# Layer 0's head of a two-layer attention and MLP kernel: a new order for the first three batches, with batch 1's second value product, batch 2's turns and three of batch 1's high halves placed behind the first raw tiles

## What is computed

```python
mod = (_silu(L0_c) @ L0_wmod).reshape(L0_c.shape[0], 6, 1, -1)
h = _layernorm(x, axis=-1) * (1 + ca) + sa
q = (x @ wq.T).reshape(B, T, H, hd)        # x is h here; k and v likewise
q, k = (rms(q), rms(k))                    # g_rms * (t * rsqrt(mean(t * t) + EPS))
q, k = (rope(q), rope(k))
scores = jnp.einsum('bhtd,bhsd->bhts', qh, kh) * scale + 1.0
attn = jax.nn.softmax(scores, axis=-1)
y = jnp.einsum('bhts,bhsd->bhtd', attn, vh)
```

## Time and profile before

| | |
|---|---|
| median of 3 runs | 1977.23 us (1971.51 to 1978.44) |
| the profiled execution | 1978.1 us, span 1976.4 us |
| mean granted clock of PE | 0.961 |
| PE busy | 1824.8 us, 92% of the span |
| DVE, ACT, POOL busy | 1338.8, 1140.3, 660.1 us |
| first raw tile, first scores | 82.25 us, 109.43 us |
| last scores of layer 0's attention | about 560 us |

### The profile page before, as it was taken

How to read it: one execution, slowest core, us unless ns; L and a number is a source line. 1 busy time by engine, 2 the same in 40 slices (tenths; PEclk the granted TensorE clock), 3 DMA queues, 4 the chain that set the end, 5 groups by cost and what they waited for, 6 DMA issues and landing times. The chain is left out here.

```text
span 1976.4 us, 29572 instructions
## 1 busy us (share of the span) xinstructions
PE 1824.8 (92%) x10382; PEld 757.2 (38%) x10382; DVE 1338.8 (68%) x2599; ACT 1140.3 (58%) x1536; POOL 660.1 (33%) x920
## 2 busy tenths in 40 slices
PE   4789999998979999999999997799999998799998
PEld 3333333332224444444444443223332322455554
DVE  5479888888834535535445352688888885689983
ACT  4368788876743424334234242577777777467674
POOL 5657777772220000000000111334433312446452
PEclk8679999999989999999999999799999999799999
DMA  3345544444243000000001003233332222433410
GB/s 119 64 93 124 131 120 115 113 102 113 92 171 148 22 1 22 22 1 22 22 0 48 1 22 65 51 77 64 74 72 59 61 54 69 158 128 133 160 43 33
DMA packets 119620, 147.65 MB, mean 75 GB/s; under 512 B 19779, under 2 KB 102838, under 8 KB 117430
## 3 DMA queue, kind: packets, MB, share of 16 engines
q1 hardware_dynamic: 119478, 145.79, 27.9%
HBM read 100.34 MB, written 45.14 MB: 74 GB/s over the span
## 5 line engine op out<-in xcount | busy, mean ns | idle before, releaser
L854 DVE TENSOR_REDUCE A_M<-A_SM 128x1 f16<-128x512 f32 x1024 | 654.1, 683 | 136.4 <-PE A_SM L1069 133.9
L625 ACT ACTIVATE A_P<-A_ST 128x1024 f32<-128x1024 f32 x512 | 523.9, 1026 | 165.7 <-PE A_ST L1085 158.0
L1069 PE MATMUL A_SM<-A_KT,A_QS 48*128 48x512 f16 x1024 | 353.0, 397 | 45.7 <-DVE A_M L854 38.1
L1627 PE MATMUL B_PA<-B_Hh,B_wh 128*128 128x512 f16 x1024 | 388.1, 379 | 0.0
L1627 PE MATMUL B_PA<-B_Hl,B_wh 128*128 128x512 f16 x1024 | 388.1, 379 | 0.0
L1546 ACT ACTIVATE B_af<-B_PA,B_sv 128x512 f32<-128x512 f32 x192 | 132.0, 688 | 353.6 <-PE B_PA L1627 353.4
L1085 PE MATMUL A_ST<-A_QS,A_KT 49*128 49x512 f16 x1024 | 299.0, 385 | 3.0 <-DMA A_QS<-A_rows 2.4
L1102 PE MATMUL A_AV<-A_P,A_V 128*32 128x512 f32 x2048 | 274.9, 609 | 4.2 <-ACT A_P L625 3.6
L1069 PEld LDWEIGHTS A_SM<-A_KT,A_QS 48*128 48x128 f16 x1024 | 83.1, 93 | 431.3 <-DVE A_M L854 381.3
L1590 DVE TENSOR_SCALAR B_Hh<-B_af 128x512 f16<-128x512 f32 x128 | 59.0, 461 | 279.3 <-ACT B_af L1546 279.3
L1341 POOL TENSOR_TENSOR B_hl<-B_hf,B_hh 128x512 f16<-128x512 f32 x14 | 16.2, 1156 | 506.2 <-ACT B_hh L1357 506.2
(11 more groups left out here) (365 smaller groups left out, 3273.2 us busy)
## 6 DMA issues: line engine op xcount, KB each, us to landing
D_w_st<-in_we_dram SPq DMA_DIRECT2D x16, 1024.0 KB, 5.0
qk<-A_tr SPq DMA_DIRECT2D x58, 256.0 KB, 2.5
A_KT<-qk SPq DMA_DIRECT2D x96, 128.0 KB, 5.1
A_QS<-qk SPq DMA_DIRECT2D x96, 128.0 KB, 4.6
A_w_st<-in_w_ffn_dram SPq DMA_DIRECT2D x32, 352.0 KB, 3.3
A_QS<-A_rows SPq DMA_DIRECT2D x512, 0.5 KB
w_hi<-A_f_hi SPq DMA_DIRECT2D x32, 176.0 KB, 3.5
w_lo<-A_f_lo SPq DMA_DIRECT2D x32, 176.0 KB, 3.8
```

The lines of the kernel that those rows point to most:

```text
L625: nc.scalar.activation(P[:, st, 2 * pair:2 * pair + 2, :], ST[:, u % 2, :, :], ACT.Exp, scale=1.0 / math.sqrt(HD)).then_inc(exp_s, 1)
L854: nc.vector.tensor_reduce(M[G % 2][:, o:o + 1], SM[:, n % 2, :], AX, ALU.max, negate=True).then_inc(max_s, 1)
L1069: nc.tensor.matmul(SM[:, n % 2, :], QS[b % 2][r, 2 * g + pair, tt * 128:tt * 128 + 128], KT[b % 2][r, 2 * g + pair, :], start=True, stop=T ...
L1627: ins = nc.tensor.matmul(out, a, c, start=start and kt == 0 and n_ == 0, stop=stop and kt == kts[-1] and n_ == len(ops) - 1)
```

## The change

Only numbers in two tables are changed. No operation is added or removed, and none changes its size or engine.

```diff
-                            H0=30, H1=31, H2=32, H3=33, HIGH=(36, 36, 36, 36, 37, 37, 37, 37), LOWS=(38, 38, 38, 38))),
-          placed(-140, dict(STAT=(10, 10, 10, 10), AGG=11, ROOT=11, XN=(16, 16, 16, 16), T0=21, T1=23, HH=(22, 24), HL=(23, 25),
...
+                            H0=24, H1=25, H2=26, H3=27, HIGH=(31, 31, 31, 31, 32, 32, 32, 32), LOWS=(33, 33, 33, 33))),
+          placed(-140, dict(STAT=(10, 10, 10, 10), AGG=11, ROOT=11, XN=(16, 16, 16, 16), T0=18, T1=19, HH=(18, 19), HL=(19, 20),
...
```

More of the change, by code:

```diff
@@ L135 @@
                             INV=(14, 17), ROT=(16, 16, 17, 17), HI=(17, 18, 19, 20), LOW=(18, 19, 20, 21),
-                            H0=30, H1=31, H2=32, H3=33, HIGH=(36, 36, 36, 36, 37, 37, 37, 37), LOWS=(38, 38, 38, 38))),
-          placed(-140, dict(STAT=(10, 10, 10, 10), AGG=11, ROOT=11, XN=(16, 16, 16, 16), T0=21, T1=23, HH=(22, 24), HL=(23, 25),
-                            QK0=25, QK1=26, QK2=27, QK3=28, V0=40, V1=42, SUM=(29, 29, 34, 35), VAR=(30, 34), RMSG=(31, 35),
-                            INV=(32, 37), ROT=(33, 36, 48, 50), HI=(37, 39, 128, 133), LOW=(38, 40, 129, 134),
+                            H0=24, H1=25, H2=26, H3=27, HIGH=(31, 31, 31, 31, 32, 32, 32, 32), LOWS=(33, 33, 33, 33))),
+          placed(-140, dict(STAT=(10, 10, 10, 10), AGG=11, ROOT=11, XN=(16, 16, 16, 16), T0=18, T1=19, HH=(18, 19), HL=(19, 20),
+                            QK0=20, QK1=21, QK2=22, QK3=23, V0=30, V1=127, SUM=(29, 29, 34, 35), VAR=(30, 34), RMSG=(31, 35),
+                            INV=(32, 37), ROT=(33, 36, 48, 50), HI=(37, 132, 133, 134), LOW=(38, 46, 133, 135),
                             H0=137, H1=139, H2=140, H3=141, HIGH=(143, 143, 144, 144, 145, 145, 146, 146), LOWS=(147, 147, 148, 148))),
-          placed(-140, dict(STAT=(35, 35, 36, 36), AGG=37, ROOT=37, XN=(41, 41, 41, 41), T0=44, T1=46, HH=(45, 47), HL=(46, 47))),
+          placed(-140, dict(STAT=(28, 28, 28, 28), AGG=28, ROOT=29, XN=(30, 30, 30, 30), T0=129, T1=131, HH=(129, 131), HL=(130, 132))),
           placed(-140, dict(STAT=(127, 128, 130, 131), AGG=132, ROOT=133, XN=(135, 136, 138, 139)))]
@@ L153 @@
 LAST_AT = dict(LOADS=246, SPLIT0=256, SPLIT1=257)
-MOD_AT = (-138, -134, -106)
+MOD_AT = (-138, -134, -111)
 OWN_BANK0 = {("T0", 0): "X", ("T1", 0): "AV", ("V0", 0): "SM0", ("V1", 0): "SM1"} | {(f"QK{i}", n): f"ST{i}" for i in range(4) for n in range(2)}
```

## The result

The changed kernel takes 1983.67 us in the median of 20 runs (1977.57 to 1993.34), against 1976.34 us before in the same job (20 runs, 1969.74 to 1986.13). The ratio is 1.0033, with a 95% interval of 1.0019 to 1.0046: 6.5 us slower, between 3.8 and 9.1 (the two medians alone lie 7.3 apart). The profiled execution has a span of 1978.7 us.

What follows compares the result with a forecast made beforehand. PE was taken to bound the steady part, so the first scores' shift reaches the end one to one: 1978.1 + 6.5 = 1984.6, with the median 0.9 lower, predicted 1984 us; forecast range 1981 to 1988.

Steps and rivals of the forecast that it cites:

- Step 1: Batch 1's turns behind fewer HI: H turns at 49.5, copies done at 52.6, 8.2 us earlier.
- the rule of the Trainium skill's page: GpSimd reading SBUF holds up two-input DVE instructions; batch 1's copies would end up to 1.9 us later.
- Step 2: Key and query loads wait for batch 2's XN: first load at 60.6, token load costs 0.5, data at 76.3.
- Step 3: Raw tiles ahead of V1 and batch 2's turns: they start at 76.3 instead of 82.25, 5.9 us earlier.
- Step 4: Batch 1's HI of tokens 1 behind batch 2's turns delays POOL's rotations and HL: QK0 at 101.7, 6.5 us later.
- Step 5: From batch 2's QK0 to the first scores, lists unchanged: 14.24 us, so first scores at 115.9 instead of 109.43.
- The lead: Rival: the raw tiles' earlier start carries through to the end, -5.9 us, 1971; chance 0.09.
- The clock rival: PE's idle before QK0 prolongs half clock beyond first scores, losing 5 us more: 1989; chance 0.20, shared with held-up rotations.
- the gap from 68 to 75: PE's half clock behind this gap was said to agree with the rule that gaps drop the clock.

Runs made afterwards that it cites:

- e2: Changed kernel with batch 2's XN at 34 instead of 30, so batch 3's token load stands behind the twelve loads; 1973.45 us, ratio 0.9986.
- e3: Changed kernel with batch 1's HI of tokens 1 at 39 and batch 2's XN at 34; 1968.50 us (0.9957), once more 1972.65 us (0.9969).
- e1: Changed kernel with HI of batch 1's tokens 1 back at 39 instead of 132, ahead of batch 2's turns; 1973.52 us, ratio 0.9985.
- e7: Changed kernel with batch 2's T1 two positions later, HI of tokens 1 behind it, and batch 3's ROOT at 135 instead of 133; ratio 1.0041.

## Why the prediction was right, and where its terms were off

The time came out at 1983.67 us for the 1984 predicted, and 6.5 us above before for 6.5. The prediction put what a measurement can tell at 0.5%; the interval of this one reaches 0.13% to either side, so that the 0.33% are told from no change.

*What bounds.* The steady part did not give the lateness back: the first scores moved by 6.5 us, those at position 128 from 344.2 to 350.2. The last pair moved by less, from 559.67 to 563.52. The two profiles differ there in the clock: between 440 and 470 us PE was granted 0.89 before and 1.00 after, as the last row of the windows above and this one of before show:

```profile
...
440.00:470.00 30.00, 25.54 (x172) 6.89 (x164) 25.70 (x48) 17.99 (x20) 9.01 (x8) 0.89 0.57 156
...
```

That this clock is what closed the gap from 6.0 to 3.9 us was not tried. The spans of the two profiles (2.3 us apart) say less than the 20 runs of each kernel.

*Step 1* held (here and below the predicted number stands in brackets): second half of QK0 at 41.94 (42.0), H turns at 49.31 (49.5), copies done at 52.48 (52.6). The 42.0 does not follow from its terms: from 39.0 they add up to 42.7, or to 41.5 if LOW runs beside the way out. In the trace LOW started at 39.62, as soon as POOL was done with the first HL, which the sum leaves out. So 42.0 was in part luck. The last HI came at 48.53 instead of 46.40: 0.3 us of the 2.1 were there already at T0 (35.41 against 35.11), and 1.8 came on DVE, which was held up beside the HL and LOW on POOL. It was not the rotations that took longer but three small instructions ahead of one (38.57 to 41.97 in DVE's timeline): 2.7 us, less 0.8 that a rotation piece beside a LOW had paid there before. 1.8 us is the size that the rule of the Trainium skill's page "SBUF — State Buffer", section "Who interferes with whom", gave with the trace's price (1.9). But it delayed HI and LOW while PE was busy with QK, and so cost PE only the 0.88 us that it waited at H0.

*Step 2* held in its main part: first of the twelve loads at 59.99 (60.6). The price of the token load ahead of them was 0.9 to 1.3 us rather than 0.5: from the first issue to the last landing it is 16.5 us, where the twelve took 15.2 before. In e2, which has no token load ahead of them, it was 15.6 (the last issued at 58.99, 10.1 to landing). Start of the raw tiles 76.57 (76.3).

*Step 3* held: 5.7 us (5.9).

*Step 4* was the right mechanism with a term 2 us too small. T1 of batch 2 ran 11.4 us behind the first raw tile (87.95 - 76.57), where I had 9.6. V1 held the pairs back by 2.4 us where I had 1.5, and T0 by 0.8 where I had put nothing. The links behind T1 came as summed: two rotations 10.1 us, QK0 15.7 us behind T1's start (15.8).

*Step 5* was off by as much the other way. From QK0 to the first scores it took 12.3 us instead of 14.24. The clock is the difference that the rows show. The stretch from QK0 to the first scores, before and in the changed kernel:

```profile
...
95.19:109.43 14.24, 11.38 (x41) 3.74 (x40) 9.10 (x16) 4.83 (x9) 4.92 (x11) 0.50 0.15 41
...
```

```profile
...
103.64:115.95 12.31, 8.86 (x38) 3.14 (x39) 8.14 (x13) 4.24 (x8) 5.96 (x12) 0.78 0.18 52
...
```

It took 14.2 us where PE was granted 0.50 (before, e3), 13.8 where it was 0.62 (e1, e7), and 12.3 where it was 0.78 (the changed kernel, e2, e3 once more). As e3 stands at both ends, the order of the instructions does not decide it. So that first scores came out at 115.95 for 115.9 is two errors of 2 us that cancel, and luck. The 6.5 us of the time rest on 20 runs and have an interval of 2.6 to either side.

*The rivals.* The lead was not kept. Nor is it all there to be had: in e1, with the first raw tile 4.9 us ahead of before (77.32), the first scores come only 1.9 us ahead, since V1 and the turns among the raw tiles cost PE 3.4. The clock rival came true in a small part. The windows around the rise of the clock, after and before:

```profile
...
124.00:128.00 4.00, 4.00 (x17) 0.79 (x15) 1.81 (x4) 2.35 (x4) 3.92 (x4) 0.56 0.01 1
128.00:132.00 4.00, 4.00 (x30) 1.09 (x26) 3.20 (x6) 2.84 (x4) 2.16 (x3) 1.00 0.44 120
...
```

```profile
...
116.00:119.50 3.50, 3.50 (x11) 0.94 (x10) 2.08 (x5) 1.02 (x1) 3.42 (x4) 0.50 0.21 70
119.50:124.00 4.50, 4.50 (x31) 1.30 (x34) 3.58 (x6) 3.84 (x6) 4.07 (x5) 1.00 0.03 6
...
```

PE is granted full speed from 119.5 us on before, and in the changed kernel from about 128, some 8 us later, as against 6.5 of the first scores. So the rise came later than the shift by less than 2 us, not by the further 10 us at half clock that the rival priced, and the ratio shows no loss beyond the 6.5. What moved QK0 was the chain: e1 takes the late HI away and the wait for POOL goes with it.

The trace of before bears out less than the prediction says of the gap from 68 to 75. The value products behind the gap ran at half clock, but those ahead of it did so already, with PE busy all the time:

```profile
...
66.00:68.00 2.00, 1.98 (x10) 1.06 (x8) 1.79 (x12) 0.00 (x0) 0.04 (x1) 0.50 1.13 134
...
```

*What stays open.* What decides where the full clock falls between QK0 and the first scores, and with it up to 2 us of their start, no run here shows. Nor was step 1 measured alone in the kernel before.

## What to carry to other kernels

When an instruction is moved in an in-order list, follow it to who waits for it, then to what stands behind that waiter in its own list, and go on until the chain ends at the engine that binds: here one rounding on ACT held two rotations on POOL, and these an unrelated batch's low half that TensorE needed. A gain that does not show is often taken by a load that now stands ahead of others in a queue and waits for something else: look at what the queue's next entry waits for. And where the head's first scores move the end nearly one to one, their start in a profile shows shifts that 12 timed runs do not tell apart. But two profiles of one kernel can differ by 2 us in the steps ahead of it, so take a second profile before you trust less than that.

## What was not expected of the hardware

Small two-input operations on DVE are held up beside POOL as much as large ones. The three instructions of 64 columns took 1.18, 1.08 and 1.08 us (38.57, 39.78 and 40.89 in DVE's timeline of the changed kernel). Before, the same three took 0.22, 0.23 and 0.23, the first of them here:

```profile
...
38.27 0.22 DVE L781 TENSOR_TENSOR A_rln<-A_rln 128x64 f32<-128x64 f32 x1
...
```

POOL ran an HL, a LOW and an HL beside them in the changed kernel:

```profile
...
38.05 1.61 POOL L535 TENSOR_TENSOR A_hl<-A_hf,A_hh 128x512 f16<-128x512 f32 x1 [0.74 <-ACT A_hh L699]
39.62 1.15 POOL L505 TENSOR_TENSOR A_qkl<-A_qo,A_qkh 128x512 f16<-128x512 f32 x1
40.74 1.15 POOL L535 TENSOR_TENSOR A_hl<-A_hf,A_hh 128x512 f16<-128x512 f32 x1
...
```

Each DVE instruction ends within 0.1 us of the end of the one on POOL (39.75 and 39.66, 40.86 and 40.77, 41.97 and 41.89). So the price was set by how long POOL took, not by the size of DVE's work: 2.7 us for the three together. A rotation piece of 256 columns paid 0.97.
